# Moving the channel product of a graph-attention layer from ScalarE to GpSimd, with a new order of the work in a slot

## The reference, cut to what matters

```python
alpha = relu(bn(einsum('bchw,oc->bohw', x, wa)))      # 32 channels, "query"
sigma = relu(bn(einsum('bchw,oc->bohw', x, ws)))      # 32 channels, "key"
att = softmax(where(adj, einsum('bkn,bkm->bnm', af, sf), NEG), axis=2)
h_s = einsum('bnm,bcm->bcn', att, xf)
Gc = einsum('bcn,bdn->bcd', xf, xf)
catt = softmax(where(cadj, Gc, NEG), axis=2)          # only c-1 and c+1 are not 0
h_p = einsum('bcd,bdn->bcn', catt, xf)
out = (1 - gama) * x + gama * elu(h_s + h_p)
```

## Time and profile before

| | |
|---|---|
| median of 3 runs | 604.75 us (601.31 to 605.41) |
| profiled execution | 608.46 us, its span 606.7 us |
| mean granted TensorE clock | 0.904 |
| busy: DVE | 380.1 us (63%), 669 instructions |
| transfers | 102.28 MB, queue busy 58.0% |
| from the first `catt` (55.9 us) to the last (573.7 us) | 15 images |

### The profile page before, as it was taken

The page is one execution under the profiler, slowest core; times in us unless marked ns, Lnnn a source line. Parts: engine busy times, 40 slices in busy tenths (PEclk is TensorE's granted clock), DMA queues, the critical chain, the costliest instruction groups (busy, mean ns, idle before and its releaser), DMA issues.

```text
span 606.7 us, 18825 instructions
## 1 busy us (share of the span) xinstructions
PE 492.1 (81%) x7621; PEld 385.8 (64%) x7684; DVE 380.1 (63%) x669; ACT 429.2 (71%) x1043; POOL 233.9 (39%) x140
## 2 busy tenths in 40 slices
PE   0468989888898888979798888989798997888783
PEld 0236677666767575767667575767667686675672
DVE  3213576665857666675857676675857676584872
ACT  0244678758877777858777777868877777787683
POOL 5200044334424442444334442444334442443365
PEclk9995997979899898979999898979999797889877
DMA  8990055765666567655766567655767477523113
GB/s 234 241 244 15 3 169 145 210 191 154 179 190 191 165 188 209 199 168 166 199 179 193 161 200 209 193 178 166 196 190 208 126 210 204 178 87 124 71 71 139
DMA packets 55702, 102.28 MB, mean 169 GB/s; under 512 B 6208, under 2 KB 6464, under 8 KB 55616
## 3 DMA queue, kind: packets, MB, share of 16 engines
q1 hardware_dynamic: 55616, 101.07, 58.0%
HBM read 34.20 MB, written 33.55 MB: 112 GB/s over the span
## 4 chain that ended last, share of the span: by engine, by line
PE 49%; DVE 24%; issue 13%; ACT 12%; DMA 2%; SPq 1%; POOLq 0%; DVEq 0%; ACTq 0%
PE z L439 17%; PE gb L439 13%; DVE z L361 9%; PE xp L449 8%; PE score L439 7%; ACT probs L263 5%; DVE gram_d L385 4%; PE et L525 4%; ACT z L278 3%; DVE neg_max L339 3%; DVE gram_e L380 2%; ACT upper L235 2%; DMA const<-constants_dram 2%; DVE probs_t L354 1%; DVE probs L346 1%
## 5 line engine op out<-in xcount | busy, mean ns | idle before, releaser
L214 POOL TENSOR_TENSOR blend<-elu,blend 128x1024 f32<-128x1024 f32 x64 | 150.8, 2356 | 360.7 <-ACT elu L290 360.7
L439 PEld LDWEIGHTS z<-probs_t,upper 64*128 64x128 f32 x2304 | 165.1, 201 | 76.5 <-issue 75.1
L439 PE MATMUL z<-probs_t,upper 64*128 64x128 f32 (+1 forms) x2304 | 182.6, 295 | 36.1 <-DVE z L361 34.1
L449 PE MATMUL xp<-const,x 128*128 128x128 f32 x512 | 94.9, 314 | 44.7 <-ACT upper L235 37.6
L361 DVE SCALAR_TENSOR_TENSOR z<-near,catt,z 128x512 f32<-128x512 f32 x128 | 91.8, 752 | 61.8 <-ACT z L278 61.7
L263 ACT ACTIVATE probs<-score,neg_max 128x128 f32<-128x128 f32 x256 | 90.5, 371 | 55.2 <-DVE neg_max L339 55.2
L278 ACT ACTIVATE z<-x,vec,catt 128x512 f32<-128x512 f32 x128 | 94.6, 773 | 10.2 <-DVE catt L393 9.9
L235 ACT ACTIVATE upper<-xp 128x512 f32<-128x512 f32 x128 | 76.0, 594 | 32.3 <-PE xp L449 28.4
L449 PEld LDWEIGHTS xp<-const,x 128*128 128x128 f32 x512 | 62.1, 157 | 57.5 <-issue 50.7
L366 DVE SCALAR_TENSOR_TENSOR elu<-elu,z 128x512 f32<-128x512 f32 x128 | 81.8, 680 | 14.7 <-ACT elu L285 14.7
L439 PE MATMUL score<-key,query 32*64 32x64 f32 (+1 forms) x1536 | 78.3, 247 | 13.9 <-issue 5.8
(11 more groups left out here) (49 smaller groups left out, 253.5 us busy)
## 6 DMA issues: line engine op xcount, KB each, us to landing
x<-x_dram SPq DMA_DIRECT2D x64, 512.0 KB, 6.2
out_dram<-blend SPq DMA_DIRECT2D x64, 512.0 KB, 4.1
near<-x SPq DMA_DIRECT2D x128, 224.0 KB, 5.0
near<-x SPq DMA_DIRECT2D x128, 30.0 KB, 4.6
const<-constants_dram SPq DMA_DIRECT2D x1, 435.5 KB, 10.2
const<-constants_dram SPq DMA_DIRECT2D x1, 128.0 KB, 2.1
wt<-w_dram SPq DMA_DIRECT2D x1, 64.0 KB, 3.4
vec<-vectors_dram SPq DMA_DIRECT2D x1, 5.5 KB, 3.1
```

Of the source, the lines that this page charges most:

```text
L214: nc.gpsimd.tensor_tensor(blend[s % BLENDS][:, :, :], elu[s % 2][:, :, :], blend[s % BLENDS][:, :, :], ALU.add).then_inc(blend_done, 1)
L439: return nc.tensor.matmul(o, l, r, start=start, stop=stop, skip_group_check=True, **kw)
L449: last = nc.tensor.transpose(xp[:, v * C + h * P:v * C + (h + 1) * P], xb[:, h, at0:at0 + WIN], ident)
```

## The change

ACT's weigh_own is gone. POOL makes the same products, into a new SBUF tile `product` (two buffers), after keep_x of the same step and ahead of add_elu of the step two before it. VectorE's mix reads `near` and `product`, both in SBUF, and writes z, where it read `near` from SBUF and z from PSUM before; the wait for elu_out of step s-2 moves from ACT's product to this mix. The bias of exp(z-1) is an immediate -1.0 and no longer a column of `vec`, and the constant 1.0 of the product is an immediate too. ACT, VectorE and PE do the parts of a slot in a new order.

```diff
+            def weigh_own(s):
+                b, q = s // QUARTERS, s % QUARTERS
+                pool.wait_ge(catt_done, b + 1)
+                if s >= 2:
+                    pool.wait_ge(mix_done, 2 * (s - 2) + 2)
+                for h in range(HALF):
+                    nc.gpsimd.tensor_scalar(product[s % 2][:, h, :], xs[b % XBUFS][:, 1 - h, cols(q)],
+                                            catt[:, h, 1 - h:2 - h], 1.0, ALU.mult, ALU.add).then_inc(product_done, 1)
...
                 if real(t - 1):
                     keep_x(t - 1)
+                    weigh_own(t - 1)
                 if real(t - 3):
                     add_elu(t - 3)
...
-                nc.scalar.activation(elu[s % 2][:, h, :], z[s % 2][h][:, :], ACT.Exp, bias=vec[:, V_MINUS:V_MINUS + 1])\
+                nc.scalar.activation(elu[s % 2][:, h, :], z[s % 2][h][:, :], ACT.Exp, bias=-1.0)\
...
-                zh = z[s % 2][h]
-                nc.vector.scalar_tensor_tensor(zh[:, :], near[b % 2][:, h, q * QN:(q + 1) * QN], catt[:, h, h:h + 1],
-                                               zh[:, :], ALU.mult, ALU.add).then_inc(mix_done, 1)
+                if s < 2:
+                    dve.wait_ge(z_open, 1)
+                else:
+                    dve.wait_ge(elu_done, 2 * (s - 2) + h + 1)
+                nc.vector.scalar_tensor_tensor(z[s % 2][h][:, :], near[b % 2][:, h, q * QN:(q + 1) * QN],
+                                               catt[:, h, h:h + 1], product[s % 2][:, h, :],
+                                               ALU.mult, ALU.add).then_inc(mix_done, 1)
```

The order in ACT's loop over slots:

```diff
-                if b + 1 < B:
-                    move_xt(b + 1, q, 0)
                 for h in range(HALF):
                     if real(t - 3):
                         exp_z(t - 3, h)
+                if b + 1 < B:
+                    move_xt(b + 1, q, 0)
+                if q == 2 and b + 1 < B:
+                    move_query(b + 1)
+                if q == 3 and b + 1 < B:
+                    move_key(b + 1)
+                if real(t - 3):
+                    times_gama(t - 3)
+                if q == 1 and 0 <= b < B:
+                    exp_gram(b)
                 if real(t):
                     exp_scores(t)
                 if b + 1 < B:
                     move_xt(b + 1, q, 1)
```

In VectorE's loop:

```diff
+                for h in range(HALF):
+                    if real(t - 3):
+                        elu_out(t - 3, h)
                 if q == 1 and 0 <= b < B:
                     gram_softmax_in(b)
                 if real(t):
                     maxima(t)
-                for h in range(HALF):
-                    if real(t - 3):
-                        elu_out(t - 3, h)
+                if real(t - 1):
+                    move_probs(t - 1)
                 if q == 1 and 0 <= b < B:
                     gram_softmax_out(b)
+                if q == 0 and 0 <= b < B:
+                    gram_pick(b)
                 if real(t):
                     normalise(t)
-                if q == 0 and 0 <= b < B:
-                    gram_pick(b)
-                if real(t - 1):
-                    move_probs(t - 1)
                 for h in range(HALF):
                     if real(t - 1):
                         mix_channels(t - 1, h)
```

In PE's loop, where the projections of the next image come a slot earlier and its halo earlier in the slot:

```diff
                 if real(t - 1):
                     transpose_probs(t - 1)
-                if q == 2 and b + 1 < B:
+                if q == 1 and b + 1 < B:
                     if b < 0:
                         pe.wait_ge(const_in, 48)
                     project_query(b + 1)
+                if q == 2 and b + 1 < B:
+                    project_key(b + 1)
                 if q == 3 and b + 1 < B:
-                    project_key(b + 1)
+                    edges(b + 1)
                 if real(t - 2):
                     z_sums(t - 2, 1)
                 if q == 0 and 0 <= b < B:
                     shift_gram(b)
-                if q == 3 and b + 1 < B:
-                    edges(b + 1)
```

More of the change, by code:

```diff
@@ L35 @@
 C_ALL = C_MASK + MASKS
-V_GAMA, V_ONE, V_MINUS = 8, 9, 10
+V_GAMA = 8
 def graph_attention(nc, x, w_t, vectors, constants, out):
@@ L68, in graph_attention @@
         wt = sb("wt", [P, HALF, 2 * HID])
-        vec = sb("vec", [P, 11])
+        vec = sb("vec", [P, 9])
         bn = sb("bn", [P, 8, 2])
@@ L87, in graph_attention @@
         catt = sb("catt", [P, 2, 2])
+        product = [sb(f"product{i}", [P, HALF, QN]) for i in range(2)]
         elu = [sb(f"elu{i}", [P, HALF, QN]) for i in range(2)]
@@ L269, in exp_gram @@
                 nc.scalar.activation(gram_x[:, :, :], gram_d[:, :, :], ACT.Exp).then_inc(gram_exp, 1)
[L271 to L279, removed]
             def exp_z(s, h):
@@ L306, in _ @@
                     move_xt(b + 1, q, 1)
-                if q == 1 and 0 <= b < B:
-                    exp_gram(b)
-                if q == 2 and b + 1 < B:
-                    move_query(b + 1)
-                if q == 3 and b + 1 < B:
-                    move_key(b + 1)
-                for h in range(HALF):
-                    if real(t - 1):
-                        weigh_own(t - 1, h)
-                if real(t - 3):
-                    times_gama(t - 3)
                 if q == 3 and b + 1 < B:
@@ L623 @@
     norms = np.stack([a[n + s] for s in "as" for n in "gbmv"], axis=1)
-    vectors = np.concatenate([np.tile(norms, (QUARTERS, 1)), np.tile(a["gama"].reshape(1, 1), (P, 1)),
-                              np.tile(np.array([[1.0, -1.0]], np.float32), (P, 1))], axis=1)
+    vectors = np.concatenate([np.tile(norms, (QUARTERS, 1)), np.tile(a["gama"].reshape(1, 1), (P, 1))], axis=1)
     arrays = {"x_dram": a["x"], "w_dram": w_t, "vectors_dram": vectors, "constants_dram": shape_constants()}
```

## The result

The changed kernel is slower: 642.99 us as a median of 4 runs (635.35 to 646.13) against 605.08 us before, a ratio of 1.059 (95% interval 1.048 to 1.071). The sign was forecast, the size was not: 619 was predicted and 634 was the end of the range. The profiled execution was the quickest of the four, 635.35 us with a span of 633.6. Some executions of a kernel are slowed as a whole, so every ratio with an interval is taken over the undisturbed ones alone and can differ from the quotient of two medians, which are over all.

A forecast was written before the change was run, and what follows sets the result against it. A ring of PE, ACT and VectorE was taken to set the pace. Images of 35.4 us against 34.5 gave +13.5, start -1, end +2: 608.5 + 14.5 = 623 profiled, 619 median; range 538 to 634, likeliest case 605 to 634.

The forecast's parts named there:

- The exclusion in both directions: VectorE instructions with two SBUF inputs and POOL instructions reading SBUF each wait for the whole of the other; 619 us median.
- The first rival: VectorE keeps its place, only its first instruction is held, PE is the bound; 540 us median, chance 0.25.
- the second: POOL is not held by VectorE at all, keep_x ends at 4.85; 577 us median, chance 0.13.
- POOL's products, 0.6 us (0.45 to 0.75): Each of POOL's two added tensor_scalar of 512 columns per slot, taken as half of a 1.2 us one.
- Gama again at 8.15: From ACT's product with gama to the next in q=2 and q=3: 8.15 us a slot (7.9 to 8.4).
- The rule that I took from one row: Between POOL and VectorE, the place passes at each instruction's end to who is waiting, taken to hold in both directions.
- q=0, 9.5 us: First slot of an image: PE's 6.08 us, then copy 0.6, gram_pick 0.5, reciprocal and division 0.8, mixes 1.35.
- q=1, 9.0 us: Second slot: catt at 13.3, products, division and mix 0 in turns, then POOL's add before mix 1, ending at 18.5.
- The full-clock image, 34.8: Sum of an image's four slots without the cost of slow-clock passages: 34.8 us (34.0 to 35.6).
- The same 0.6: Slow-clock cost per image, from the average before lying 0.6 us above the image shown; gives 35.4 us.
- Start -1 and end +2: Outside the 15 images: one wait saved at the start, -1 us; last three slots longer by the ring's length, +2.
- nothing on the path: Immediate bias saves 0 to 85 ns on each of 128 exponentials, where ACT has slack; at most 0.17 us a slot otherwise.

The follow-up runs named there:

- the fillers: The changed kernel plus matmuls of 512 columns, computing nothing used, which PE does where it waits for the mix; 605.7 us.
- the mix free: The changed kernel, but the mix reads z in PSUM as second input instead of the product tile; 598.9 us, 0.986.
- the control with fillers: The kernel before plus unused matmuls where PE waits for the mix (3 in q=0, 6 in q=2); 586.6 us, 0.972.
- the fastest kernel: The changed kernel's order, but ACT makes the products into z and POOL's add_elu also waits for the division; 556.8 us, 0.913.

## Why the prediction was right or wrong, point by point

- **The exclusion in both directions, the forecast's mechanism: right.** The first rival (VectorE keeps its place throughout) and the second (POOL is not held, which the prediction once calls the third) are refuted by keep_x at 2.13 us and the mix at 1249 ns; the sign of the whole hung on it. Without the second SBUF input the kernel is 44 us faster. VectorE's busy time rose by 28 us and not by the 80 forecast: mix and division have 74 more, but the small softmax instructions lost 36 that the prediction left out, although it read one of them held for 2.37 us.
- **"POOL's products, 0.6 us (0.45 to 0.75)":** 0.69 undisturbed.
- **"Gama again at 8.15":** 7.54 at full clock. Mix 0 does keep its place behind the division, and product 0 comes after mix 1. The rule that I took from one row held in q=1 and not in q=2 and q=3, which saves one product in the chain.
- **q=0, 9.5 us:** 8.63. The 6.08 us that I read for PE contained a stop of 0.7 us in the Gram band that is not in every image; read from one image, it went into the sum as fixed.
- **q=1, 9.0 us:** 8.84, with the add between the mixes as said.
- **The full-clock image, 34.8:** 32.65. Too long by 2.1.
- **"The same 0.6" for the clock: this is the step that failed.** It was 36.3 - 32.65 = 3.7 us per image in the profiled execution. The prediction took the clock's price from the kernel before as if it were a constant, though it named longer waits of PE in two slots of four. Of these 3.7 us, 2.3 are in the eleven ordinary images (34.9 on average), in which the clock falls behind the waits for the mix, mostly for 3 to 7 us at a time. The other 1.4 come from the four long images, with 10 to 17 us at half speed at a stretch; in three of them a stop of 1.3 to 2.3 us without a releaser stands in the Gram band. That PE's standing still is what costs the clock is shown by the fillers; why it costs so much more here than in the kernel before is only partly shown, since with the mix free and no longer waits the clock was 0.866. Besides, 0.6 was only the difference between the average image and a good one, which itself was at a clock of 0.95; the control with fillers shows that the kernel before paid more as well: 33.1 us per image with them, against 34.5.
- **Start -1 and end +2:** together -0.4.
- **The sum:** 15 x (36.3 - 35.4) - 1.4 = +12 to the 623 forecast for a profiled execution, which is the 635 measured. The other three executions lay at 641 to 646 with clocks of 0.836 to 0.843, below the 0.852 of the profiled one; so the median is 24 above the prediction in place of 12.
- **The immediate bias and the removal of ACT's products, "nothing on the path" and "helps":** the bias is worth nothing (0.999), as said. The removal does not help by itself: on POOL, with the mixes free, the products still leave the kernel slower than on ACT (0.986 against 0.959). The new order, which I costed only inside the ring, is by itself a gain of 4%.

## What to carry to other kernels

A VectorE instruction with two SBUF inputs and a GpSimd instruction that reads SBUF hold each other up from both sides, and the profile shows it only as longer instructions: compare their means with undisturbed ones before moving work to GpSimd, and keep one input of VectorE in PSUM, or make GpSimd wait until VectorE's instruction is through. Where TensorE waits more, count its clock too, and do not carry its price over from the kernel before: take a full-clock image and a slow one from the trace and ask which the change will make more frequent. Here the price per image went from 1.4 us or more to 3.7, and it did not follow the sum of the waits alone.

## What the runs showed of the hardware that was not expected

- GpSimd held by VectorE: keep_x 2.13 us in place of 1.19. Behind a division that had itself been held, VectorE's next instruction went first (0.76 us, not held) when GpSimd's was keep_x, of 1024 or of 512 columns, and second when it was a product of 512 columns.
- 256 added matmuls made the changed kernel 37 us faster (643 to 606) by its clock, 0.852 to 0.964. In the fastest kernel, whose clock was 0.95 without any, 128 made it 16 us slower (557 to 573).
- The exponential from PSUM takes 595 ns with an immediate bias and 679 with a column of SBUF.
- PE stops of 1.3 to 3.6 us without a releaser, mostly in the run of short matmuls of the Gram band. In the changed kernel each of the three lies in a stretch at 1.2 GHz; with fillers, images with such a stop of 1.65 and 1.68 us had a mean clock of 1.00.
